# A decoder's front in another order: loads, norms and casts moved around memory and cross attention

## The reference, cut to what matters

```
x = x + mem(layernorm(x))            # gelu(xn @ W_K.T @ W1.T) @ W2.T
x = x + cross(layernorm(x), ctx)     # one head: softmax((xn Wq + bq)(ctx Wk + bk)^T / 16) (ctx Wv + bv)
x = x + layers(layernorm(x))         # 6 layers: local attention (16 heads, window 64), gated feed-forward
```

## Time and profile before

| | us |
|---|---|
| median of 3 runs | 3038.22 (3037.7 to 3038.64) |
| the profiled execution | 3044.19 |
| its span | 3042.4 |
| PE busy | 2809.6 (92%) |
| DVE, ACT, POOL busy | 2401.1 (79%), 2171.6 (71%), 1741.5 (57%) |
| end of front, start of the layers' block | 152.0 |

### The profile page before, as it was taken

The page is one execution under the profiler, slowest core; times in us unless marked ns, Lnnn a source line. Parts: engine busy times, 40 slices in busy tenths (PEclk is TensorE's granted clock), DMA queues, the critical chain, the costliest instruction groups (busy, mean ns, idle before and its releaser), DMA issues. The chain is left out here.

```text
span 3042.4 us, 81409 instructions
## 1 busy us (share of the span) xinstructions
PE 2809.6 (92%) x26408; PEld 2475.6 (81%) x26408; DVE 2401.1 (79%) x7761; ACT 2171.6 (71%) x6102; POOL 1741.5 (57%) x1556
## 2 busy tenths in 40 slices
PE   7679999999999999999999999999999999999996
PEld 5558888888888888888888888888888888888885
DVE  3568888888888888888888888888888888888883
ACT  3357777777777778777777877777777777777772
POOL 3355665655666555666656566565656665555550
PEclk9879999999999999999999999999999999999997
DMA  3202221333321134132233213233221332310110
GB/s 125 89 21 82 77 68 64 125 101 108 101 75 68 64 134 139 61 101 75 68 133 126 79 61 103 73 128 116 85 76 61 103 119 69 97 28 25 36 25 19
DMA packets 140064, 251.68 MB, mean 83 GB/s; under 512 B 14718, under 2 KB 78728, under 8 KB 138632
## 3 DMA queue, kind: packets, MB, share of 16 engines
q1 hardware_dynamic: 139912, 249.76, 25.0%
HBM read 137.72 MB, written 80.55 MB: 72 GB/s over the span
## 5 line engine op out<-in xcount | busy, mean ns | idle before, releaser
L880 PE MATMUL project<-w_qkv,xT 128*128 128x512 f32 x3456 | 917.4, 404 | 10.6 <-ACT v L1054 8.4
L880 PEld LDWEIGHTS project<-w_qkv,xT 128*128 128x128 f32 x3456 | 614.8, 189 | 131.5 <-ACT v L1054 15.1
L1101 ACT ACTIVATE probs<-probs,shift 128x128 f32<-128x128 f32 x1536 | 598.1, 393 | 126.4 <-DVE shift L1319 123.9
L1153 POOL TENSOR_SCALAR sums_sq<-sums_sq 128x8 f32<-128x8 f32 x384 | 222.0, 578 | 707.3 <-DVE sums_sq L1246 699.3
L1319 DVE CUSTOM_DVE_ANT_0 probs<-score,mask,query_scale 128x128 f32<-128x128 f32 x1536 | 442.8, 347 | 151.2 <-PE score L972 149.1
L935 PE MATMUL wide<-nT,w_up 128*128 128x256 f32 x3456 | 477.0, 288 | 85.6 <-DVE gates L1289 76.1
L935 PEld LDWEIGHTS wide<-nT,w_up 128*128 128x128 f32 x3456 | 451.4, 193 | 115.7 <-DVE gates L1289 87.6
L1331 DVE TENSOR_SCALAR probs<-probs,sums 128x128 f32<-128x128 f32 x1536 | 477.5, 373 | 13.8 <-DVE sums L1327 0.2
L1159 POOL TENSOR_TENSOR query_scale<-sums_sq,half 128x8 f32<-128x8 f32 x192 | 374.6, 1951 | 22.1 <-POOL sums_sq L1153 12.1
L1162 POOL TENSOR_TENSOR sums_sq<-sums_sq,half 128x8 f32<-128x8 f32 x192 | 372.4, 1939 | 16.0
L1108 ACT COPY probsT<-turned 128x512 f32<-128x512 f32 x384 | 225.1, 586 | 215.2 <-issue 128.6
(11 more groups left out here) (120 smaller groups left out, 4908.5 us busy)
## 6 DMA issues: line engine op xcount, KB each, us to landing
w_parts_scratch<-staging SPq DMA_DIRECT2D x120, 519.0 KB, 2.7
staging<-in_w_next SPq DMA_DIRECT2D x60, 519.0 KB, 4.9
w_qkv<-w_parts_scratch SPq DMA_DIRECT2D x20, 1536.0 KB, 9.3
v_mid<-v SPq DMA_DIRECT2D x192, 128.0 KB, 2.3
w_up<-w_parts_scratch SPq DMA_DIRECT2D x20, 682.0 KB, 6.3
y_in<-y_scratch SPq DMA_DIRECT2D x48, 256.0 KB, 3.0
res<-y_scratch SPq DMA_DIRECT2D x48, 256.0 KB, 2.7
y_scratch<-res SPq DMA_DIRECT2D x40, 256.0 KB, 3.2
```

The source lines that it names most:

```text
L880: last = pe.matmul(project[(x - 1) % 2][:], xT[a][:, h, t * P:(t + 1) * P], w_qkv[w][:, h, c, g, :], start=(h == 0 and (a, w) == PASSES[0] ...
L1101: last = act.activation(probs[:, k, cols], probs[:, k, cols], ACT.Exp, bias=shift[:, k, i:i + 1], scale=-1.0, accum_out=sums[:, k, i:i + 1])
```

## The change

The loads for the fold (identity, wk_mem, w1t_mem) are issued by ACT, with a semaphore of their own; SP's order is another; x is waited for one by one, the contexts by quad. Quad 1's contexts are loaded as soon as quad 0's V is made; blocks 3 and 4 are staged behind quad 0's x2 stores. ACT casts behind the GELUs and behind the probabilities' copies. Norm (1,0) is made ahead of quad 0's scores, and GpSimd's low parts of block 2 go behind it. The adds of the mix are made inside norm 2, each ahead of its own statistics. PE gets a wait: hidden of quad 1 waits for quad 0's adds (same banks). `y_in` and its semaphore move to the outer program, and its first load to the front. Only one column of xT is cleared, and the table scaling goes ahead of the first rotation. The first wait of PE's reads is for seven loads, the mask among them.

```diff
 @block.sync
+            for k in range(QUAD):
+                sp.dma_start(x[k][:], as_tiles(D["x"][k])).then_inc(x_in[k], 16)
+            sp.dma_start(w2t_mem[:], D["mem_w2t"]).then_inc(weights_in, 16)
+            for dst, src in ((wk, "cross_wk"), (wq, "cross_wq"), (wv, "cross_wv")):
...
+            for k in range(QUAD):
+                load_context(k)
             sp.dma_start(bqk[:], D["cross_bqk"]).then_inc(weights_in, 16)
             sp.dma_start(bv[:], D["cross_bv"].broadcast_to([P, DIM])).then_inc(weights_in, 16)
+            W.stage(sp, 0)
+            for k in range(QUAD, BATCH):
+                sp.dma_start(x[k][:], as_tiles(D["x"][k])).then_inc(x_in[QUAD], 16)
+            sp.dma_start(T["mask"][:], D["mask"]).then_inc(weights_in, 16)
+            for blk in (1, 2):
+                W.stage(sp, blk)
+            sp.wait_ge(kv_ready, 2 * QUAD)
+            for k in range(QUAD, BATCH):
                 load_context(k)
...
             for i in range(QUADS):
...
+                if i == 0:
+                    for blk in (3, 4):
+                        W.stage(sp, blk)
...
+                if i == 0:
+                    sp.wait_ge(y_stored, 16 * QUAD)
+                    sp.dma_start(T["y_in"][:], as_tiles(D["y"][0])).then_inc(T["y_loaded"], 16)
+                    W.stage(sp, len(WEIGHT_PIECES) - 1)
 @block.tensor
-            pe.wait_ge(weights_in, 16 * 10)
+            pe.wait_ge(fold_in, 16 * 3)
...
                     pe.wait_ge(turned_out, (i * 2 + 0) * QUAD + j + 1)
+                    if i > 0:
+                        pe.wait_ge(cross_added, (i - 1) * QUAD + j + 1)
...
+                if i == 0:
+                    pe.wait_ge(weights_in, 16 * 7)
 @block.scalar
+            act.dma_start(ident[:], D["ident"]).then_inc(fold_in, 16)
+            for dst, src in ((wk_mem, "mem_wk"), (w1t_mem, "mem_w1t")):
+                act.dma_start(dst[:], D[src].rearrange("(k p) n -> p k n", p=P)).then_inc(fold_in, 16)
...
-                for piece in range(WEIGHT_PIECES[3 * i]):
-                    W.split_high(act, 3 * i, piece)
                 for j in range(QUAD):
                     act.wait_ge(hid_ready, i * QUAD + j + 1)
                     act.activation(hidT[j][:], bank[j][1][0:MEMORY, 0, :], ACT.Gelu).then_inc(hid_act, 1)
+                for piece in range(WEIGHT_PIECES[3 * i]):
+                    W.split_high(act, 3 * i, piece)
 @block.gpsimd
-                for blk in {(0, 0): (0,), (0, 1): (1, 2), (0, 2): (3,), (1, 1): (4, 5)}.get((i, s), ()):
+                for blk in {(0, 0): (0,), (0, 1): (1,), (1, 0): (2,), (0, 2): (3,), (1, 1): (4, 5)}.get((i, s), ()):
 @block.vector
-                    layer_norm(0, 0, lambda j: dve.wait_ge(x_in[0], QUAD * 16))
+                    layer_norm(0, 0, lambda j: dve.wait_ge(x_in[j], 16))
...
+                if i == 0:
+                    layer_norm(1, 0, lambda j: dve.wait_ge(x_in[QUAD], QUAD * 16))
...
-                for j in range(QUAD):
+                def add_cross(j):
                     k = i * QUAD + j
...
                     last.then_inc(cross_added, 1)
-                if i == 0:
-                    layer_norm(1, 0, lambda j: dve.wait_ge(x_in[1], QUAD * 16))
-                layer_norm(i, 2, lambda j: dve.wait_ge(cross_added, i * QUAD + j + 1))
+                    dve.wait_ge(cross_added, k + 1)
+                layer_norm(i, 2, add_cross)
 layers
-                if s.early:
+                if s.early and not (isinstance(n, int) and n == -1):
...
-                pool.memset(xT[part][:].bitcast(FP32), 0.0).then_inc(cleared, 1)
+                pool.memset(xT[part][:, 1, 0:1].bitcast(FP32), 0.0).then_inc(cleared, 1)
...
-                if isinstance(s.n, int) and s.n == -1:
-                    build_tables(0)
                 for item in DVE_ORDER:
+                    if isinstance(s.n, int) and s.n == -1 and item == ("rotate", 0, 0):
+                        build_tables(0)
```

More of the change, by code:

```diff
@@ L354, in front @@
                 for j in range(QUAD)]
-        weights_in = sem("f_weights_in")
-        x_in, ctx_in = [sem(f"f_x_in{i}") for i in range(2)], sem("f_ctx_in")
+        fold_in, weights_in = sem("f_fold_in"), sem("f_weights_in")
+        x_in = [sem(f"f_x_in{k}") for k in range(QUAD)] + [sem("f_x_in_rest")]
+        ctx_in = [sem(f"f_ctx_in{i}") for i in range(BATCH // QUAD)]
         folded_ready, folded = sem("f_folded_ready"), sem("f_folded")
@@ L461, in _ @@
                 for j in range(QUAD):
-                    pe.wait_ge(ctx_in, (i + 1) * QUAD * 16)
+                    pe.wait_ge(ctx_in[i], QUAD * 16)
                     for m in range(HALVES):
@@ L546, in _ @@
                     last.then_inc(probs, 1)
-                for piece in range(WEIGHT_PIECES[2 + 3 * i]):
-                    W.split_high(act, 2 + 3 * i, piece)
                 for j in range(QUAD):
@@ L551, in _ @@
                     act.copy(prT[j][:], bank[j][0][:]).then_inc(probs_out, 1)
+                for piece in range(WEIGHT_PIECES[2 + 3 * i]):
+                    W.split_high(act, 2 + 3 * i, piece)
         @block.gpsimd
@@ L649, in layers @@
         tables = sb("tables", [P, 4, TILES, HEAD_DIM])
-        y_in = sb("y_in", [P, TILES, DIM])
+        y_in = T["y_in"]
         xT = [sb(f"xT{s}", [P, HALVES, TOKENS + 2], FP32R) for s in range(2)]
@@ L692, in layers @@
         cleared, mid_loaded = sem("cleared"), sem("mid_loaded")
-        y_loaded, res_loaded, y_stored = sem("y_loaded"), sem("res_loaded"), sem("y_stored")
+        y_loaded, res_loaded, y_stored = T["y_loaded"], sem("res_loaded"), sem("y_stored")
         filled, act_read, dve_read = sem("filled"), sem("act_read"), sem("dve_read")
@@ L1367, in decoder_kernel @@
             "half": ctx.enter_context(nc.sbuf_tensor("half", [P, GROUP_HEADS], FP32)),
+            "y_in": ctx.enter_context(nc.sbuf_tensor("y_in", [P, TILES, DIM], FP32)),
+            "y_loaded": ctx.enter_context(nc.semaphore("y_loaded")),
         }
```

19 lines of the change are left out of this document (3 added, 16 removed).

## The result

The change took **3001.0 us** (median of four runs, 2999.7 to 3003.3), beside 3038.2 for the kernel before on the same chip: a ratio of 0.9874, 95% interval 0.986 to 0.9887. Its profiled execution has a span of 2999.2 us at a mean granted clock of 0.984; that of before had 3042.4.

The account below looks back on a forecast made before the run. PE was taken as the chain in the front, so each closed gap should reach the end. Terms summed to 30.6 us, taken from the 3038.2 median: forecast 3007.6 us, range 3002 to 3013.

Parts of the forecast that it names:

- The start (7.1): Start of the front: quad 0's reads begin at 21.6 instead of 28.68, held by the mask's load; 7.1 us gained.
- The clock at the reads (0, between +3.5 and -1.7): Quad 0's reads and K: same low-clock loss as before, 0; bounds 3.5 us gained and 1.7 lost.
- Quad 0's norms (0): Second quad's first norms, 6.6 us on VectorE, are covered by its 7.94 us wait for quad 0's scores; no cost.
- copies (1.9): Probabilities' copies go ahead of w_out's casts on ACT: PE's waits of 1.9 us in quad 0 and 1.4 in quad 1 go.
- norms between the quads (6.5): Between quad 0's mix and quad 1's hidden: tiles normalised already, PE turns at its own pace; 6.5 us gained.
- contexts (6.4 + 1.5): Quad 1's contexts loaded earlier: the 6.4 us wait before K goes, and K at full clock gains 1.5 us.
- last norms (1.9): End of the front: fewer statistics steps behind the last add, from 7.5 us to about 5.6; 1.9 us gained.
- w_up's low parts (-0.8): GpSimd's low parts delay quad 1's second norms: 0.8 us lost, bounds 0 and 2.5 lost.
- Start of the layers (4.2): Layers' first block: early first tile, less clearing, table scaling moved to the first rotation; first unit 4.2 us sooner.
- PE's clock stays high: Rival at quad 0's reads: mask does not bind or clock stays high; about 3002 to 3004 us, chance 0.17.
- Closed gaps open next to themselves: Rival: VectorE or GpSimd late for quad 1's second norms or quad 0's scores, layers' start keeps 1 us; 3010 to 3014, chance 0.22.
- The code's fetch: Slower rival: moved layers' loops meet one more late instruction fetch each pass; 3047 us at 1.1 us a pass, chance 0.02.

Follow-up runs that it names:

- the filled pair: The change and the kernel before, each with 14 unread matrix products ahead of PE's wait for the gates in every slot: 3001.9 and 3035.1 us.
- r1: The change run once more, unaltered, with a second trace: 3005.1 us, ratio 0.989.

## Why the prediction was right, and where it failed

**The start (7.1).** Right in mechanism and size: 7.4 at the reads, with the mask's load in the brackets. The version with the mask first shows it as the bound, not only as the last name. **The clock at the reads (0, between +3.5 and -1.7).** The end -1.7 came in the profiled execution: V shifted by 5.7, the reads by 7.4. It is a draw too: from the reads to V the traces have 12.4, 15.7 or 17.4 us with the old order, 13.9, 15.7 or 17.4 with the new one.

**Quad 0's norms (0), copies (1.9), norms between the quads (6.5), contexts (6.4 + 1.5), last norms (1.9).** Right, together and where undone, each in one execution: 8.0 to 9.7 for the 8.4 of the norms, 6.0 to 7.7 for the 7.9 of the contexts, where PE's wait and K's slowness alone are 8.2. Transposes did not let the clock fall: hidden behind 1.91 us of them takes 3.67 at full clock, against the page of the Trainium skill weighed in the prediction.

**w_up's low parts (-0.8).** Wrong: they cost nothing. The load took 6.9 us from issue (70.62) to its cast (77.51), the early end of the 7 to 9 that I had, and GpSimd was through 3.9 us before the turns.

**Start of the layers (4.2).** 4.05 between the two traces, 4.5 with it undone, 4.0 with it alone. The times gave 5.6 and 5.8 with it undone and alone; what is over is not explained, and within the draw.

**The step that failed** is the sentence "all of it should reach the end, because nothing behind 160 us is changed and the layers are a chain that begins with PE's first unit", and with it the step from the profiled execution to the median, "6.0 below". Same code was taken for same length. The layers are a chain, but its length is drawn anew in each execution: 30 waits of 2.2 us, behind 12 to 16 of which the clock falls (14 traces), at 1.6 us each, and a tail of 38 to 46 us, longer with more low clock in it. The 77 executions of the kernel before lie over 17 us. The median before lay at the mean of its draw (3038.2 and 3038.4); the four measured after lay 2.4 below theirs (3001.0 and 3003.4). Of the 37.2 us, then, 2.2 are which executions were measured. Over many it is 35.0; with the draw in the layers taken out it is 33.5, of which 32.0 are in the front by the first unit. What is left between 33.5 and 35 is the layers' draw falling a little better in the change, which no run explains, and it is within what 9 executions can tell. So the 6.6 us between 37.2 and the sum's 30.6 are 2.2 and 1.5 of draws, 1.5 between the first unit and the end of the filled pair, and 1.4 in the front, 0.8 of them the term for w_up: the sum itself was a little too small, by less than what the draws added.

The range failed for the same reason. It was made of rivals about the front alone, with nothing for the executions' own spread, though the profiled execution standing 6 us above runs that agreed to 1 was a hint of it. The rival "PE's clock stays high" had its time about right (3002), but in the result's profiled execution the clock fell; in r1's it stayed high, without a wait for the mask, and that execution took 3003.7. "Closed gaps open next to themselves" happened once, and where it was not looked for: PE waits for VectorE's second norms, 1.5 us, whenever the clock stays up at the reads. The code's fetch did not show either: slots of equal work have the same two lengths on both sides.

## What to carry to other kernels

Put the sum at the last changed instruction, where it can be tested, and then ask whether the unchanged rest has a fixed length: compare one row per loop pass over one execution, and if passes of equal work come in two lengths, the end of the program is a draw and the range must hold it. A gap of PE costs more than its own length when the clock falls behind it; if the gap itself can't be closed, matrix work that nobody reads closes it for the clock, and is to be put only where PE truly idles, since a wait of about 0.4 us filled with 1.9 us of work cost 1.0. And parts of a change are not to be priced alone: an order on ACT that cost 3.3 us by the waits of the kernel before cost 17 us at the first unit once the rest had moved.

## What I had not expected of the hardware

- The same wait, 2.23 us, with the same work behind and ahead of it, let the clock fall in some passes and not in others: 12 to 16 of 30 in 14 profiled executions, in different slots from one to the next. With 0.6 us of it left, not once in 30, in any of the five filled traces.
- In the kernel before, a mean granted clock of 0.976 over 3042.4 us makes some 146 us at the low level, behind the first 20 us or so for which the trace has no record. At half the speed that is 73 us or 2.4% of the span, more than it costs, since PE idles in part of it. The Trainium skill (TensorE: Matmul & The Clock Gate, "What's actually happening") calls the number of slow matmuls run-variable, with which the traces agree, and puts the ramp's penalty, that of the slow start alone, at under 1% of a typical kernel. Here most of the loss lies behind the start, and some 15 us of it could be had back.
- The change with the filling in every slot issues 27080 matmul records for 26408, at a mean granted clock of 0.989 for 0.984, in the same time.
